# A local transformer stage that projects the values instead of weighing the tokens

## What is computed

```python
def attn_layer(x, Wqkv, qs, ksc, Wo):            # x: (16, 256, 128)
    q, k, v = jnp.split(x @ Wqkv, 3, -1)         # 16 heads of 64: 1024 columns each
    ...                                          # l2norm, scales, rotary positions on q and k
    out = local_attention(q, k, v)               # windows of 32; each looks at itself and the window before
    return out.transpose(0, 2, 1, 3).reshape(b, n, INNER) @ Wo
for i in range(6):
    x = attn_layer(shift_tokens(x), Wqkv[i], q_scale[i], k_scale[i], Wo[i]) + x
    x = ffn_layer(shift_tokens(x), ln_g[i], ln_b[i], W1[i], b1[i], W2[i], b2[i]) + x
```

## Time and profile before

| | us |
|---|---|
| median of 3 runs | 5458.0 (5451.22 to 5475.68) |
| the profiled execution: time | 5460.38 |
| the profiled execution: span of the core | 5458.6 |
| TensorE busy in the span | 4901.9 |
| VectorE, ScalarE, GpSimd busy | 3871.1, 3358.3, 2655.1 |
| the stage of the change, from 1325 to 4715: TensorE busy | 3219.32 of 3390 |

### The profile page before, as it was taken

How to read it: one execution, slowest core, us unless ns; L and a number is a source line. 1 busy time by engine, 2 the same in 40 slices (tenths; PEclk the granted TensorE clock), 3 DMA queues, 4 the chain that set the end, 5 groups by cost and what they waited for, 6 DMA issues and landing times. The chain is left out here.

```text
span 5458.6 us, 130392 instructions
## 1 busy us (share of the span) xinstructions
PE 4901.9 (90%) x50569; PEld 3344.9 (61%) x50569; DVE 3871.1 (71%) x6444; ACT 3358.3 (62%) x5923; POOL 2655.1 (49%) x1681
## 2 busy tenths in 40 slices
PE   6888557996999999999999999999999999799897
PEld 4444234664777667776776677767776777566543
DVE  5999796775777677776777677767776777477553
ACT  5676323554666666666666666666666666455444
POOL 4777110001566556655665666555665666266200
PEclk8999777998999999999999999999999999899899
DMA  3121000001000100010001000100001000000020
GB/s 85 62 77 62 4 0 7 2 2 29 12 11 11 30 14 12 12 31 14 12 12 29 13 12 12 31 15 12 12 12 31 12 12 12 14 2 2 24 63 20
DMA packets 76241, 113.89 MB, mean 21 GB/s; under 512 B 22496, under 2 KB 53424, under 8 KB 72048
## 3 DMA queue, kind: packets, MB, share of 16 engines
q1 hardware_dynamic: 67744, 110.60, 7.4%
q10 hardware_dynamic: 8256, 0.03, 0.1%
HBM read 70.38 MB, written 2.49 MB: 13 GB/s over the span
## 5 line engine op out<-in xcount | busy, mean ns | idle before, releaser
L2218 POOL TENSOR_TENSOR lt_qk<-lt_qk,lt_rot 128x1024 f32<-128x1024 f32 x384 | 907.0, 2362 | 205.1 <-DVE lt_rot L2582 205.1
L2228 POOL TENSOR_TENSOR lt_prob<-lt_prob,lt_total 128x1024 f32<-128x1024 f32 x192 | 365.2, 1902 | 1086.2 <-DVE lt_total L2604 1086.2
L2223 POOL TENSOR_TENSOR lt_qk<-lt_qk,lt_rnorm 128x1024 f32<-128x1024 f32 x384 | 726.4, 1902 | 110.5 <-ACT lt_rnorm L2458 103.0
L2265 PE MATMUL lt_ps<-lt_w_qk,lt_xs 128*128 128x512 f32 x1536 | 748.1, 610 | 22.4 <-DMA lt_scales<-in_L_scales 11.4
L2317 PE MATMUL lt_ps<-lt_z,lt_fold 128*128 128x256 f32 x3072 | 678.8, 379 | 1.7 <-ACT lt_z L2486 1.7
L2317 PEld LDWEIGHTS lt_ps<-lt_z,lt_fold 128*128 128x128 f32 x3072 | 585.0, 190 | 120.6 <-ACT lt_z L2486 24.8
L2579 DVE TENSOR_TENSOR lt_qk<-lt_ps,lt_table 128x1024 f32<-128x1024 f32 x384 | 468.2, 1219 | 76.1 <-ACT lt_sq L2448 69.1
L2582 DVE TENSOR_TENSOR lt_rot<-lt_ps,lt_table 128x512 f32<-128x512 f32 x768 | 490.6, 680 | 0.0
L2594 DVE TENSOR_REDUCE lt_nmax<-lt_ps 128x16 f32<-128x1024 f32 x192 | 229.4, 1195 | 360.1 <-PE lt_ps L2285 360.1
L2589 DVE TENSOR_REDUCE lt_norm<-lt_sq 128x16 f32<-128x1024 f32 x384 | 463.9, 1208 | 0.1
L2265 PEld LDWEIGHTS lt_ps<-lt_w_qk,lt_xs 128*128 128x128 f32 x1536 | 272.5, 193 | 251.8 <-issue 245.3
(11 more groups left out here) (409 smaller groups left out, 9845.7 us busy)
## 6 DMA issues: line engine op xcount, KB each, us to landing
mb_bs<-mb_rows SPq DMA_DIRECT2D x16, 1536.0 KB, 7.7
lt_xw<-lt_xw SPq DMA_DIRECT2D x192, 128.0 KB, 2.3
mb_bs<-mb_rows SPq DMA_DIRECT2D x16, 512.0 KB, 4.3
mo_gate_b<-mo_rows SPq DMA_DIRECT2D x16, 512.0 KB, 5.8
lt_xs<-h SPq DMA_DIRECT2D x96, 64.0 KB, 1.9
lt_w_qk<-in_L_ffn_Wqkv SPq DMA_DIRECT2D x6, 1024.0 KB, 5.2
lt_xs<-h SPq DMA_DIRECT2D x96, 63.8 KB, 1.9
lt_wvT<-in_L_wvT SPq DMA_DIRECT2D x6, 512.0 KB, 7.3
```

Source lines behind the costliest of these rows:

```text
L2218: pool.tensor_tensor(qk[:, u, :, :], qk[:, u, :, :], rot[:, u % 2, :, :], ALU.add).then_inc(sg["added"], 1)
L2223: pool.tensor_tensor(qk[:, u, :, :], qk[:, u, :, :], rnorm[:, u, :, :].to_broadcast([P, H, DH]), ALU.mult).then_inc(sg["qk"], 1)
L2265: last = pe.matmul(AT[u][:, 512 * k:512 * k + 512], xs[:, m.j, c:c + P], w_qk[:, a, 512 * k:512 * k + 512], start=True, stop=True)
```

## The change

- `project_v` projects the values at the item's front: two token tiles times 1024 columns, 4 matmuls of 512 columns, with `w_qkv` holding all three parts of the weights. ScalarE copies them to `v_tok` (`values_out`).
- `values_moved` on SyncE's queue places them by 16 transfers per item in `vw`: for each head and each window the 64 tokens that it looks at, on the right row half. It waits until all items before have been mixed.
- `mix` takes the place of `weigh`: 64 matmuls a call, 128 per item, each with 64x64 weights (one head's values) and 32 columns, in four tiles of the array; ScalarE's copies fall from four (`weighed`) to two (`mixed_out`).
- `attend` has 8 matmuls with the plain `wo` in place of 16 with `fold`. `fold`, `wvT`, `turn_x`, `xw` and the waits for `folded` and `b_up` at the layer's start are gone. `wo` is loaded by 8 transfers with the back weights.
- The PSUM parts X0 to X3 are handed out anew. Both `turn_p` stand ahead of the first `mix`; `centre`, `var` and the `turn_qk` alternate; VectorE does `rotate(m, 3)` behind `attended(n)`; GpSimd has `unit_length(m, 1)` ahead of `rotated(m, 2)`.

```diff
--- before.py
+++ after.py
...
-        z = sb("z", [P, 2, WINDOWS, 8, WIN])
-        parts = z[:, :, :, :, :].rearrange("p a w i q -> p (a w i q)").rearrange("p (k w) -> p k w", k=8)
-        ln = AdaNorm(core, ctx, sg, 1, SHIFT_B, SCALE_B, [parts[:, 0:2, :], parts[:, 2:6, :]])
+        v_tok = sb("v_tok", [P, 2, 2, H // 2, DH])
+        att = sb("att", [P, 2, H // 4, S])
+        ln = AdaNorm(core, ctx, sg, 1, SHIFT_B, SCALE_B,
+                     [att[:, 0, :, :].rearrange("p j s -> p (j s)").rearrange("p (k w) -> p k w", k=2),
+                      v_tok[:, :, :, :, :].rearrange("p t k i d -> p (t k i d)").rearrange("p (k w) -> p k w", k=4)])
-        w_qk = sb("w_qk", [P, 2, INNER])
-        wvT = sb("wvT", [P, H // 2, P])
-        wo = sb("wo", [P, H // 2, P])
-        fold = sb("fold", [P, 2, H // 2, P])
...
+        w_qkv = sb("w_qkv", [P, 3, INNER])
+        wo = sb("wo", [P, 2, H // 4, P])
...
-            def other_halves(m):
-                sp.wait_ge(sg["xw"], m.n + 1)
+            def values_moved(m):
+                sp.wait_ge(sg["v_out"], 2 * m.n + 2)
                 sp.sem_inc(sg["fetch_step"], 1)
-                sp.wait_ge(sg["z_made"], 8 * m.n)
+                sp.wait_ge(sg["mixed"], 8 * m.n)
+                sp.sem_inc(sg["fetch_step"], 1)
                 for k in range(2):
-                    sp.dma_start(xw[64 - 64 * k:P - 64 * k, 1, :, :], xw[64 * k:64 * k + 64, 0, :, :]).then_inc(sg["xw_moved"], 16)
+                    for s in range(2):
+                        r = 64 * k + WIN * s
+                        for q in range(4):
+                            w = q + 1 - s
+                            count = 1 if w == 4 else 2
+                            sp.dma_start(vw[r:r + WIN, w:w + 4 * count - 3:4, :, :].rearrange("p w i d -> p w (i d)"),
+                                         v_tok[WIN * q:WIN * q + WIN, 0:count, k, :, :].rearrange("p t i d -> p t (i d)")
+                                         ).then_inc(sg[f"v_moved{k}{s}"], 16)
...
+                heads = T["L1_ffn_Wo"][one, :, :].rearrange("l (j e a d) n -> d e a (l j) n", e=4, a=2, d=DH)
+                for k in range(2):
+                    for a in range(2):
+                        for r, e in ((0, 3 * k), (64, 2 - k)):
+                            sp.dma_start(wo[r:r + 64, k, 2 * a:2 * a + 2, :], heads[:, e, a, :, :]).then_inc(sg["back_in"], 16)
...
+            def project_v(m, t, to):
+                c = WIN + P * t
+                for k in range(2):
+                    last = pe.matmul(to[:, 512 * k:512 * k + 512], xs[:, m.j, c:c + P], w_qkv[:, 2, 512 * k:512 * k + 512],
+                                     start=True, stop=True)
+                last.then_inc(sg["v_proj"], 1)
...
-            def weigh(m, i, to):
-                t, pair = i // 2, i % 2
-                for w in (2 * pair, 2 * pair + 1):
-                    for k in range(2):
-                        r, c = 64 * k, 512 * k + 256 * (w % 2)
-                        copy, i_w = window(4 * t + w, k)
-                        last = pe.matmul(to[:, c:c + 256], xw[r:r + 64, copy, i_w, :],
-                                         probT[r:r + 64, t, :, WIN * w:WIN * w + WIN], start=True, stop=True, tile_position=(r, 0))
-                        if w % 2 == 1:
-                            last.then_inc(sg["z_made"], 1)
-
-            def attend(m, half):
-                for i in range(4 * half, 4 * half + 4):
-                    for k in range(2):
-                        slot = 2 * i + k
-                        last = pe.matmul(attn, fold[:, slot // 8, slot % 8, :], z[:, k, :, i, :], start=(slot == 0), stop=(slot == H - 1))
-                if half == 1:
-                    last.then_inc(sg["attn_out"], 1)
+            def mix(n, t, to):
+                pe.sem_inc(sg["mix_step"], 1)
+                for half in range(0, H // 2, 2):
+                    for w, i, k in itertools.product(range(4), (half, half + 1), range(2)):
+                        r, c = 64 * k, 64 * ((i + k) % 2)
+                        o = 512 * k + P * (i // 2) + WIN * w
+                        last = pe.matmul(to[c:c + 64, o:o + WIN], vw[r:r + 64, 4 * t + w, 2 * (i % 4) + i // 4, :], probT[r:r + 64, t, i, WIN * w:WIN * w + WIN],
+                                         start=True, stop=True, skip_group_check=True, tile_position=(r, c))
+                        if w == 3 and half == H // 2 - 2:
+                            last.then_inc(sg["mixed"], 1)
+
+            def attend(n):
+                for k in range(2):
+                    for j in range(H // 4):
+                        last = pe.matmul(attn, wo[:, k, j, :], att[:, k, j, :], start=(k + j == 0), stop=(k == 1 and j == H // 4 - 1))
+                last.then_inc(sg["attn_out"], 1)
...
                 if m:
-                    project(m, 0)
+                    pe.wait_ge(sg["gelu"], m.n - 1)
+                    project(m, 0, PT[0])
+                    pe.wait_ge(sg["qkT"], 4 * m.n)
+                    project_v(m, 0, X1)
+                    pe.wait_ge(sg["s_read"], 2 * m.n)
+                    project_v(m, 1, X3)
                 if n:
-                    pe.wait_ge(sg["s_read"], 2 * n.n + 2)
-                    turn_p(n, 0, X2)
+                    if m:
+                        pe.wait_ge(sg["v_out"], 2 * m.n + 1)
+                    else:
+                        pe.wait_ge(sg["qkT"], 4 * n.n + 4)
+                    turn_p(n, 0, X1)
                 if m:
-                    project(m, 1)
+                    pe.wait_ge(sg["y_ffn"], B + m.n - 1)
+                    if not opens(m):
+                        pe.wait_ge(sg["b_up"], m.l + 1)
+                    project(m, 1, PT[1])
                 if n:
-                    pe.wait_ge(sg["xw_moved"], 32 * n.n + 32)
                     pe.wait_ge(sg["pT"], 2 * n.n + 1)
-                    weigh(n, 0, X2)
-                    weigh(n, 1, X3)
+                    turn_p(n, 1, X1)
+                    for k in range(2):
+                        for s in range(2):
+                            pe.wait_ge(sg[f"v_moved{k}{s}"], 64 * n.n + 64)
                     if m:
                         pe.wait_ge(sg["qk_read"], 4 * m.n + 1)
                     else:
-                        pe.wait_ge(sg["ffn_h"], n.n)
-                    turn_p(n, 1, X1)
+                        pe.wait_ge(sg["gelu"], n.n)
+                    mix(n, 0, X2)
+                if m:
+                    pe.wait_ge(sg["v_out"], 2 * m.n + 2)
+                    project(m, 2, PT[2])
+                if n:
+                    pe.wait_ge(sg["pT"], 2 * n.n + 2)
+                    mix(n, 1, X1)
                 if m:
                     if n:
-                        pe.wait_ge(sg["z"], 4 * n.n + 1)
-                    project(m, 2)
+                        pe.wait_ge(sg["att"], 2 * n.n + 1)
...
+                    pe.wait_ge(sg["back_in"], 16 * BACK * (n.l + 1))
+                    pe.wait_ge(sg["att"], 2 * n.n + 2)
+                    attend(n)
...
-                    up(n, 1, X1)
+                    up(n, 1, X0)
                 if m:
-                    if n:
-                        pe.wait_ge(sg["gelu"], n.n + 1)
-                    turn_x(m, X3)
...
-                for g in range(H // 2):
-                    for k in range(2):
-                        r = 64 * k
-                        last = pe.matmul((X1, X3)[k][:, P * g:P * g + P], wvT[r:r + 64, g, :], wo[r:r + 64, g, :], start=True, stop=True,
-                                         tile_position=(r, 0))
-                        if g == H // 2 - 1:
-                            last.then_inc(sg["fold_made"], 1)
...
-                pe.wait_ge(sg["b_up"], l + 1)
-                pe.wait_ge(sg["folded"], 2 * (l + 1))
...
+            def values_out(m, t, src):
+                act.wait_ge(sg["v_proj"], 2 * m.n + t + 1)
+                if t == 0:
+                    for k in range(2):
+                        for s in range(2):
+                            act.wait_ge(sg[f"v_moved{k}{s}"], 64 * m.n)
+                act.copy(v_tok[:, t, :, :, :].rearrange("p k (j a) d -> p k j (a d)", a=2),
+                         src.rearrange("p (j k e) -> p k j e", k=2, e=2 * DH)).then_inc(sg["v_out"], 1)
...
+            def mixed_out(n, t, src):
+                act.wait_ge(sg["mixed"], 8 * n.n + 4 * t + 4)
                 act.wait_ge(sg["attn_out"], n.n)
-                dst = z[:, :, 2 * i:2 * i + 2, :, :].rearrange("p k w i q -> p k (w i q)")
-                act.copy(dst, src.rearrange("p (k c) -> p k c", k=2)).then_inc(sg["z"], 1)
+                act.copy(att[:, :, :, P * t:P * t + P].rearrange("p k j q -> p (k j) q"),
+                         src.rearrange("p (g q) -> p g q", q=P)).then_inc(sg["att"], 1)
...
                     sum_squares(m, 1)
                     rotate(m, 2)
                     sum_squares(m, 2)
-                    rotate(m, 3)
                     sum_squares(m, 3)
                 if n:
```

(25 more changed lines are left out.)

147 lines of the change are left out of this document (64 added, 83 removed).

## The result

The changed kernel takes 5739.4 us (median of 4 runs, 5738.5 to 5753.7); the kernel before, on the same chip, 5458.7. The ratio is 1.0507, with an interval of 1.0492 to 1.0522: 5.1% slower, where 2.2% was forecast. The profiled execution spans 5736.8 us against 5458.6.

What follows compares the result with a forecast made beforehand. TensorE, busy 90% of the span, was taken as the bound. From the profiled 5460.4 us, -29 (items), -33 (layer changes), +143 (late instruction fetches) and +42 (jumps) gave 5583, stated as 5580 us, 2.2% slower; range 5340 to 5800.

Steps and rivals of the forecast that it cites:

- 96 items, held: TensorE's time per item without fetch gaps: 34.0 us instead of 34.28, times 96, -29 us.
- layer's changes: Between layers: fold and the waits for folded and b_up go, 5.5 us saved six times, -33 us (0 to -51).
- edges of blocks: TensorE's loop code no longer held, so fetched late: 1.7 us on each of 84 loop items, +143 us (0 to +308).
- jumps back: End of each of 42 loop iterations, to code no longer held: 0 to 1.8 us each, taken as 1, +42 us.
- The mix: Each of an item's two runs of mix on TensorE: 1.75 us, two together 0.5 us less than the two weigh calls.
- first upper end: Upper bound for a run of mix: 2.64 us, from the 1.32 us of weight loads in scores, at twice the width.
- head: TensorE from an item's first projection to the end of attend: 19.5 us instead of 20.14.
- tail: TensorE from attend's end to the next item, held also by other engines' chain: 14.5 us instead of 14.14.
- 1: TensorE's loop body is held and the item's end is as walked: 5425 us, chance 0.12.
- 2: Body held, and dropping turn_x lets the second scores start 0.85 us earlier: 5343 us, chance 0.12.
- 3: Loop body not held but fetched in time, gaps near 0.5 us per item, none at jumps: 5440 to 5490, chance 0.12.
- Rival 4: Weight loads bind the mix: at 2.64 us a run +1.8 per item, 5755 us; at 4.1, 6030; chance 0.12.

Runs made afterwards that it cites:

- a_one: Changed kernel with TensorE's loop at one item per iteration, one token buffer and later token transfers: 5479.2 us, 1.0033 of the kernel before.
- a_unrolled: Changed kernel with TensorE's 14 loop items of each layer written out, so no jumps back in this stage: 5591.9 us, 1.0241 of the kernel before.
- a_phase: Changed kernel with 36 or 44 do-nothing instructions ahead of TensorE's loop in each layer, moving its start within a block of 256: 5713.4 us.
- a_w32: Changed kernel with only the first 32 columns of each head's values loaded as weights in mix, number of matmuls unchanged: 5637.4 us.
- a_best: Changed kernel with a one-item TensorE loop, one token buffer, and next layer's weights loaded mid-layer into a second buffer: 5453.7 us, 0.9983 of the kernel before.
- b_loop4: Kernel before with TensorE's loop alone made of four items per iteration, some 3400 instructions: 5530.5 us, 1.0130 of the kernel before.

## Why the prediction was wrong

Its mechanism was right and is shown: the body of 1698 instructions was held, the one of 2556 isn't. What was wrong is the size of three terms. The measured ones are differences of ratios, times 5460 us:

| term | forecast | measured | from |
|---|---|---|---|
| 96 items, held | -29 | +5 | items of 34.34 in a_one, 34.29 before |
| layer's changes | -33 | +13 | rest of a_one over before (18) |
| edges of blocks | +143 | +114 | a_unrolled over a_one |
| jumps back (36; 42 were counted) | +42 | +145 | after over a_unrolled |
| sum | +123 | +277 | measured in all: 281 |

**The jump** is the step that failed: "0 to 1.8 us each, I take 1". The jumps measured 4.0 us each, 145 us in place of 42, the largest part of what was missed. The upper end was taken from gaps inside `scores`. A jump back to code that isn't held is worse: 2.3 us of idle time, and then the clock, which adds 1.25 us to the first projection (3.07 for 1.82) and 0.4 to the next two (3.87 for 3.43). The trace before had such a row, at the layer's change, which was not drawn on; a projection of 1.88 us took 3.75 behind an idle stretch:

```profile
1921.66 3.75 PE L2265 MATMUL lt_ps<-lt_w_qk,lt_xs 128*128 128x512 f32 x4 [2.65 <-DVE lt_b_up L2684]
```

The mean of 4.0 hides two cases: against a_unrolled a two-item iteration is 5.0 to 6.1 us longer in layers 0 to 3, and 0.8 and 1.2 in layers 4 and 5.

**The edges** were sized fairly, 1.36 us per loop item for 1.7 (the mean of the three rows was 1.8), and the reason given, that dense code behind a wait is where fetches are late, holds: the gaps are in and behind the second `scores` in layers 0 to 3. In layers 4 and 5 they are in the first mix and at the item's start. They depend on where a block ends, as a_phase shows, which the argument from a mean of three items left out.

**The mix** was taken at 1.75 us, "a quarter above the `scores` run". It is 2.00. The nearest row had half the width of weights, and a_w32 shows that this width sets the time. It lies between what was taken and the first upper end, 2.64; twice 0.25 us in 96 items is 48 us, more than the 29 that the item was to save. The rest of the walk held: head 1506.19 to 1526.09 in a_one, 19.90 for 19.5 with the mixes 0.5 too short, tail 14.46 for 14.5, the second `scores` 11.5 us behind `attend`'s end in the changed kernel. `turn_x` gave back nothing, as said.

**The layer's change**, the second step that failed (13 us lost for 33 saved), was to save 5.5 us each, because `fold` (2.06) and its waits go. They went, but in their place the written-out code is half as long again, and its fetches meet the weights (2 MB then, 1.5 now) and, behind them, 1.92 MB of values in place of 0.25 MB of copied tokens: the gaps of 2.47 and 4.10 us in a_one, of which a_best gets 27 us back in all. A stall that is removed was priced, what was late next was not looked for.

**The rivals.** That the body is held (1 and 2) and that it is fetched in time (3) are refuted by the packets and the gaps. Rival 4 was half true: weight loads do set the mix, but the whole step is 0.5 us per item over the forecast's one and not 1.8. The transfers were priced at nothing, and in the loop that stood: the changed kernel's list of waits between 1400 and 4700 has none of a `mix` for them, and without them the kernel is some 19 us faster. The measured 5739 us lies inside the range, 5340 to 5800; the change itself was forecast at 123 us and measured at 281.

## What to carry to other kernels

Count the instructions of a loop's body on each engine before and after a change: on TensorE a float32 matmul is four, and a body that no longer lies within what is held pays for every pass, here 259 us of 281. If it must grow, shorten it by fewer items per iteration (one buffer less made that possible here) rather than write it all out. A late jump is to be priced with the clock's fall behind it, and large loads are better issued while the engine runs from held code (27 us here; in the kernel before, nothing).

## What the runs showed of the hardware

- A loop body of 2044 TensorE instructions was held when it started at the start of a block of 256 (two layers), and fetched in every pass when it started 7, 15, 23 or 31 instructions into one; 1788 was held in all layers, 2556 in none (changed kernel and a_phase).
- A jump back to code that isn't held cost 4.0 us on the mean, where all the edges of an item met in sequence cost 1.36, and what it costs depends on the start of the body: two-item iterations of 77 to 78 us on the mean against 72. The branch itself lasted 0.22 us to held code and 2.0 to 3.8 us to other code.
- In the changed kernel, after 2.32 us of idle time the granted clock was 0.65 in the 3 us from 1436; after 1.02 us it stayed at 1.00. In b_loop4, with a gap of 1.94 us before it, it was 0.54 from 1467.6 to 1470.6.
- With the 16 DMA engines 72% busy, a gap for instructions was 4.10 us long (2.20 at the same place with the load moved away); with the engines at 25% the waits of `scores` for issue were as long (1.8 us on the mean) as at 1.5% (1.9).
- A run of 128 records of 64x32 weights took 1.22 us, of 64x64 weights 2.00 us, both with 32 columns in tiles side by side.
